# Sorting both token groups of the last feed-forward part into expert blocks, with one group's blocks between the steps of the second attention

## What is computed

```python
x = x + _L0_xattn_ref(_layernorm(x, axis=-1), ctx_1024, ...)   # 16 heads
x = x + _L0_ffn_ref(_layernorm(x, axis=-1), ...)               # 32 routed experts of width 64, dense, weighted
x = x + _L1_xattn_ref(_layernorm(x, axis=-1), ctx_1024, ...)   # one head of width 128
x = x + _L1_ffn_ref(_layernorm(x, axis=-1), ...)               # 8 experts, each token takes ONE of them

# _L1_ffn_ref
ids = jnp.argmin(_dist2(xn, centroids), axis=-1)
for e in range(N_EXPERTS):
    h = jnp.einsum('bsd,dh->bsh', xn, up_w[e])                  # 128 -> 512
    a, g = jnp.split(h, 2, axis=-1)
    y = jnp.einsum('bsh,hd->bsd', a * jax.nn.silu(g), down_w[e])
    out = jnp.where((ids == e)[..., None], y, out)
return out + skip
```

## Time and profile before

| | us |
|---|---|
| time, median of 3 runs | 336.48 (334.96 to 337.52) |
| the profiled execution, its time | 338.92 |
| its span, first to last instruction | 337.0 |
| PE busy | 275.8 (82%) |
| DVE busy | 217.7 (65%) |
| ACT busy | 153.2 (45%) |
| POOL busy | 150.9 (45%) |
| mean granted clock of PE | 0.915 |

### The profile page before, as it was taken

How to read it: one execution, slowest core, us unless ns; L and a number is a source line. 1 busy time by engine, 2 the same in 40 slices (tenths; PEclk the granted TensorE clock), 3 DMA queues, 4 the chain that set the end, 5 groups by cost and what they waited for, 6 DMA issues and landing times.

```text
span 337.0 us, 4616 instructions
## 1 busy us (share of the span) xinstructions
PE 275.8 (82%) x1501; PEld 178.9 (53%) x1525; DVE 217.7 (65%) x518; ACT 153.2 (45%) x277; POOL 150.9 (45%) x173
## 2 busy tenths in 40 slices
PE   3647897799999999797799969987997996924991
PEld 1422353344444454475477746866775774813861
DVE  4824688366568565688685694477779359641872
ACT  1110034444545666654655545843455853511550
POOL 6356024113112424087487763365645366470254
PEclk9975569999999999999999998997999998985896
DMA  6798936407410220284202100200000000015100
GB/s 194 221 139 208 196 103 167 85 10 182 69 58 0 68 81 3 52 72 115 64 2 62 46 18 0 63 1 0 0 4 0 0 2 0 0 64 177 43 12 11
DMA packets 13271, 21.85 MB, mean 65 GB/s; under 512 B 1709, under 2 KB 9841, under 8 KB 12736
## 3 DMA queue, kind: packets, MB, share of 16 engines
q1 hardware_dynamic: 10976, 14.46, 19.8%
q10 hardware_dynamic: 1728, 6.29, 6.6%
q0 software_dynamic: 544, 0.81, 0.7%
HBM read 18.32 MB, written 5.11 MB: 70 GB/s over the span
## 4 chain that ended last, share of the span: by engine, by line
PE 48%; DVE 17%; DMA 10%; POOL 10%; issue 7%; ACT 5%; SPq 2%; another core or an unknown queue 0%; ACTq 0%; DVEq 0%; POOLq 0%
PE psum L1170 43%; DMA big<-qk_scratch 4%; DMA qk_scratch<-parts 3%; DVE negmax L1084 2%; DVE early L1103 2%; DVE xn L969 2%; DVE early L1109 2%; DMA pvT<-mask_k 2%; POOL out L595 2%; POOL parts L580 2%; POOL big L580 1%; ACT early L733 1%; POOL row_blocks L590 1%; DVE stats L796 1%; DMA early<-row_blocks 1%
## 5 line engine op out<-in xcount | busy, mean ns | idle before, releaser
L1170 PE MATMUL psum<-xs,ws 128*128 128x512 f32 x192 | 56.7, 432 | 0.0
L1103 DVE TENSOR_TENSOR early<-early,psum 128x512 f32<-128x512 f32 x48 | 32.7, 682 | 36.6 <-ACT early L733 36.5
L1084 DVE TENSOR_REDUCE negmax<-psum 128x4 f32<-128x1024 f32 x32 | 39.1, 1221 | 23.3 <-PE psum L1170 23.2
L733 ACT ACTIVATE early<-psum 128x512 f32<-128x512 f32 x48 | 28.8, 600 | 48.4 <-PE psum L1170 48.3
L580 POOL TENSOR_TENSOR parts<-early,parts 128x512 fp32r<-128x512 f32 x24 | 31.0, 1290 | 41.5 <-ACT parts L725 41.4
L695 ACT ACTIVATE early<-psum 128x1024 f32<-128x1024 f32 x32 | 32.7, 1024 | 31.9 <-PE psum L1170 31.9
L1170 PE MATMUL psum<-maskb,id 128*128 128x512 bf16 x115 | 39.6, 421 | 4.8 <-DVE negmax L1084 3.5
L1170 PEld LDWEIGHTS psum<-big 32*128 32x128 f32 (+1 forms) x256 | 21.0, 203 | 38.9 <-issue 30.0
L1170 PE MATMUL psum<-big 32*128 32x256 f32 (+1 forms) x256 | 35.0, 355 | 7.7 <-DMA big<-qk_scratch 7.7
L1170 PEld LDWEIGHTS psum<-xs,ws 128*128 128x128 f32 x192 | 36.7, 197 | 7.9 <-issue 0.7
L1109 DVE TENSOR_TENSOR early<-early,psum 128x512 f32<-128x512 f32 x48 | 33.0, 687 | 3.2 <-POOL big L580 1.6
(11 more groups left out here) (226 smaller groups left out, 500.4 us busy)
## 6 DMA issues: line engine op xcount, KB each, us to landing
raw<-experts ACTq DMA_DIRECT2D x12, 512.0 KB, 3.8
big<-qk_scratch SPq DMA_DIRECT2D x24, 128.0 KB
qk_scratch<-parts SPq DMA_DIRECT2D x16, 128.0 KB, 2.8
row_blocks<-fill SPq DMA_DIRECT2D x1, 1452.0 KB, 24.6
early<-row_blocks SPq DMA_DIRECT2D x1, 1056.0 KB, 5.7
big<-qk_scratch SPq DMA_DIRECT2D x16, 64.0 KB
early<-sel SPq DMA_DIRECT2D x2, 512.0 KB, 7.6
ropet<-rope SPq DMA_DIRECT2D x2, 256.0 KB, 4.8
```

The lines of the kernel that those rows point to most:

```text
L733: nc.scalar.activation(sg[:, n % 2, :], psum[:, n % 2, :], ACT.Silu).then_inc(silu_ready, 1)
L1084: nc.vector.tensor_reduce(negmax[:, b % 2, :, :].rearrange("p t (r j) -> p r t j", r=2)[:, :, :, j], psum[:, bank:bank + 2, :].rearrange(" ...
L1103: nc.vector.tensor_tensor(sg[:, n % 2, :], sg[:, n % 2, :], psum[:, 2 + n % 2, :], ALU.mult).then_inc(up_read, 1)
L1170: return nc.tensor.matmul(o, w, r, start=start, stop=stop, skip_group_check=True)
```

## The change

The 16 dense units of the last part of g0 are gone: N_DENSE is 32. Both groups are sorted now, and two sets of 11 blocks follow.

- In g1's units (n = 16..31) stands the second attention of g0, now with `rank` and four scatters behind it (SECOND, now in half units: 2u before the down product, 2u+1 after it). norm2 and norm3 stand in the same unit as the task with their statistics, where they stood one unit later.
- g0's blocks come after unit 31; between them, by BESIDE_BLOCKS, stands the whole second attention of g1, its rank and its scatters. Then g1's blocks. A block's turned tokens are made four blocks at a time (xb0, xb1, xb2).
- Two scratch tensors row_blocks, so two fills, issued one behind the other where the one stood. POOL issues 22 output scatters instead of 11; the plain store of g0's result is gone.
- Splits 12 to 23 stand in every second unit (n = 1, 3, 5, ..., 23), so that all weights are there before the blocks. The parts of the hidden values have three rooms instead of four.

```diff
-DENSE = ((0, 0), (0, 1), (1, 0))
-N_DENSE = len(DENSE) * UNITS
+N_DENSE = GROUPS * UNITS
...
+LATE_ROOMS = 18
...
-SECOND = {"yT": 3, "norm2": 4, "k1proj": 4, "xT3": 5, "q1": 6, "s1": 7, "s1_": 7, "pT": 8, "pT_": 8, "pv1": 9,
-          "oproj1": 10, "norm3": 11, "skip": 12, "xT4": 12, "dist": 13, "ohT": 14}
+SECOND = {"yT": 6, "k1proj": 7, "norm2": 7, "xT3": 9, "q1": 10, "s1": 11, "s1_": 11, "pT": 13, "pT_": 13, "pv1": 14,
+          "oproj1": 16, "norm3": 17, "skip": 18, "xT4": 19, "dist": 21, "rank": 24, "rows0": 27, "rows1": 28, "rows2": 29,
+          "rows3": 30}
+
+BESIDE_BLOCKS = ({"yT": 0, "xb0": 0, "norm2": 0, "k1proj": 1, "xT3": 2, "xb1": 3, "q1": 3, "s1": 4, "s1_": 4, "xb2": 5, "pT": 6,
+                  "pT_": 6, "pv1": 7, "oproj1": 8, "norm3": 9, "skip": 10, "xT4": 11, "dist": 12, "rank": 14, "rows0": 15,
+                  "rows1": 15, "rows2": 15, "rows3": 15},
+                 {"xb0": 0, "xb1": 1, "xb2": 3})
...
-        row_blocks = nc.dram_tensor("row_blocks", [BLOCKS * P, ROW], F32, kind="Internal").ap()
+        row_blocks = [nc.dram_tensor(f"row_blocks{g}", [BLOCKS * P, ROW], F32, kind="Internal").ap() for g in range(GROUPS)]
...
+        late = sb("late", [P, 4096])
+        raw = late[:, 0:2048].rearrange("p (a n) -> p a n", a=2)
...
+            if n % 3 < 2:
+                return parts[:, 1024 * (n % 3):1024 * (n % 3 + 1)].rearrange("p (l t) -> p l t", l=2)
+            if n < LATE_ROOMS:
+                return we[:, :, 3 * CHUNK - GT:3 * CHUNK]
+            return xs[:, :, 0:GT]
...
-            sp.dma_start(row_blocks, fill.to_broadcast([BLOCKS * P, ROW])).then_inc(filled, 16)
-            sp.wait_ge(rows_out, 64)
-            blocks_of = row_blocks.rearrange("(j p) c -> p j c", p=P)
-            sp.dma_start(row_blk[:, 0:3, :], blocks_of[:, 0:3, :]).then_inc(blocks_in0, 16)
-            sp.dma_start(row_blk[:, 3:BLOCKS, :], blocks_of[:, 3:BLOCKS, :]).then_inc(blocks_in1, 16)
-            sp.wait_ge(y0_added, 1)
-            sp.dma_start(out[0:GT, :].rearrange("(t p) d -> p t d", p=P), acc[:, 0:4, :]).then_inc(out_done, 16)
-            sp.wait_ge(out_done, 16)
+            for g in range(GROUPS):
+                sp.dma_start(row_blocks[g], fill.to_broadcast([BLOCKS * P, ROW])).then_inc(filled, 16)
+            for g in range(GROUPS):
+                sp.wait_ge(rows_out, 64 * (g + 1))
+                blocks_of = row_blocks[g].rearrange("(j p) c -> p j c", p=P)
+                sp.dma_start(row_blk[g][:, 0:4, :], blocks_of[:, 0:4, :]).then_inc(blocks_in[g][0], 16)
+                sp.dma_start(row_blk[g][:, 4:BLOCKS, :], blocks_of[:, 4:BLOCKS, :]).then_inc(blocks_in[g][1], 16)
...
+                if name.startswith("rows"):
+                    t = int(name[-1])
+                    if t == 0:
+                        pool.wait_ge(filled, 16 * GROUPS)
+                        pool.wait_ge(acc4_ready, b + 1)
+                        pool.wait_ge(place_ready, b + 1)
+                    nc.gpsimd.indirect_dma_start(row_blocks[b], bass.IndirectOffsetOnAxis(ap=place_i[:, b, t:t + 1], axis=0),
+                                                 row_tok[:, t, :], None).then_inc(rows_out, 16)
...
-                    if wi < 24 and n % 3 == 1 and (wi < 22 or n > 2 * UNITS + DOWN_LAG):
+                    if wi < 24 and n % 2 == 1:
...
+            for at in range(2 * (BLOCKS + 2)):
+                for name, b in block_tasks(0, at):
+                    late_task(name, b)
+            for g in range(GROUPS):
+                pool.wait_ge(token_ready, g + 1)
+                for j in range(BLOCKS):
+                    pool.wait_ge(blk_out, BLOCKS * g + j + 1)
...
-                if i == 22:
-
-                    act.wait_ge(y_done, 2 * UNITS)
-                ws = (ws0 if c < 3 else ws1)[:, c % 3, :, 512 * q:512 * (q + 1)]
+                if i == 23:
+
+                    act.wait_ge(y_done, LATE_ROOMS)
...
-                if n >= 4:
-                    act.wait_ge(y_done, n - 3)
+                if n >= 3:
+                    act.wait_ge(y_done, n - 2)
...
+            for g in range(GROUPS):
+                weight_at = None
+                for i in range(BLOCKS + 2):
+                    for task in block_tasks(g, 2 * i):
+                        misc_task(*task)
+                    if i == 0:
+                        weight_at = weights_of(g)
+                    if i < BLOCKS:
+                        block_up(g, i, weight_at[i])
+                    if 1 <= i <= BLOCKS:
+                        hidden_turned(BLOCKS * g + i - 1)
+                    for task in block_tasks(g, 2 * i + 1):
+                        misc_task(*task)
+                    if i >= 2:
+                        block_down(BLOCKS * g + i - 2, weight_at[i - 2])
```

More of the change, by code:

```diff
@@ L62 @@
 UP_W, DOWN_W = 2 * HID, 2 * D
+EXPERT_W = UP_W + DOWN_W
+LATE_ROOMS = 18
 SM = {}
@@ L83, in misc_uses @@
         uses += [t for t in slot_tasks(s) if t[0] in MISC_READER]
-    for stage, g in DENSE:
-        for u in range(UNITS):
-            uses += [t for t in unit_tasks(stage, g, u) if t[0] in MISC_READER]
+    for n in range(2 * N_DENSE):
+        uses += [t for t in unit_tasks(n // 2, n % 2) if t[0] in MISC_READER]
+    for g in range(GROUPS):
+        for at in range(2 * (BLOCKS + 2)):
+            uses += [t for t in block_tasks(g, at) if t[0] in MISC_READER]
     return uses
@@ L124, in tail_tasks, with unit_tasks, block_tasks @@
     return [(name, b) for name, at in TAIL.items() if s == PAIRS * b + B_START + PAIRS + 1 + at]
-def unit_tasks(stage, g, u):
-    tasks = []
-    if stage == 0 and g == 0:
-        for b in range(B):
-            tasks += tail_tasks(SLOTS + u, b)
-    if (stage, g) in ((0, 1), (1, 0)):
-        tasks += [("rank" if (name, g) == ("ohT", 0) else name, g ^ 1) for name, at in SECOND.items() if u == at]
-    return tasks
+def unit_tasks(n, late):
+    g, u = n // UNITS, n % UNITS
+    if g == 0:
+        return [task for b in range(B) for task in tail_tasks(SLOTS + u, b)] if late else []
+    return [(name, 0) for name, at in SECOND.items() if at == 2 * u + late]
+def block_tasks(g, at):
+    return [(name, g if name.startswith("xb") else 1) for name, when in BESIDE_BLOCKS[g].items() if when == at]
 def misc_index(task):
@@ L361, in build @@
         for u in range(UNITS):
-            for name, b in unit_tasks(0, 0, u):
+            for name, b in unit_tasks(u, 1):
                 if name == "oproj":
@@ L578, in _ @@
+            for n in range(N_DENSE):
+                for late in range(2):
+                    for name, b in unit_tasks(n, late):
+                        late_task(name, b)
                 if n < LOW_ON_DVE:
@@ L738, in _ @@
                     hidden_high(n - 1)
-                if u == DOWN_LAG - 1 and n > UNITS:
-                    k = n // UNITS - 1
-                    act.wait_ge(y_done, UNITS * (k + 1))
-                    if k >= 1:
-                        act.wait_ge(misc_full, misc_index(("yT", k - 1)) + 1)
+                if n == UNITS + DOWN_LAG - 1:
+                    act.wait_ge(y_done, UNITS)
                     nc.scalar.copy(yT[:, :], psum[:, 5, :]).then_inc(y_evicted, 1)
-                for name, b in unit_tasks(stage, g, u):
-                    misc_task(name, b)
+                for late in range(2):
+                    for name, b in unit_tasks(n, late):
+                        misc_task(name, b)
@@ L1444, in hidden_turned, with weights_of @@
-            def hidden_turned(j):
-                pe.wait_ge(blk_hid, j + 1)
-                if j >= 2:
-                    pe.wait_ge(blk_hlo, j - 1)
+            def weights_of(g):
+                pe.wait_ge(weight_ready, g + 1)
+                return nc.values_load_multi_w_load_instructions(
+                    weight_i[0:1, g, :], engines=(mybir.EngineType.PE,), min_val=0, max_val=(E1 - 1) * EXPERT_W,
+                    skip_runtime_bounds_check_because="clamped to the last expert where it is stored")[1]
@@ L1481, in weights_at @@
-            def weights_at(which, top):
-                return nc.values_load_multi_w_load_instructions(weight_i[0:1, which, :], engines=(mybir.EngineType.PE,),
-                                                                min_val=0, max_val=top,
-                                                                skip_runtime_bounds_check_because="clamped to the last expert before it is stored")[1]
-            up_at, down_at = weights_at(0, (E1 - 1) * UP_W), weights_at(1, (E1 - 1) * DOWN_W)
-            pe.wait_ge(hidden_ready, N_DENSE)
```

441 lines of the change are left out of this document (196 added, 245 removed).

## The result

The changed kernel takes 356.51 us at the median of four runs (354.98 to 358.18), the kernel before beside it 337.0 us (334.96 to 337.63): a ratio of 1.059, with a 95% interval from 1.052 to 1.066. It is slower by 5.9%. The profiled execution spans 353.8 us, where that of before spans 337.0.

What follows compares the result with a forecast made beforehand. PE's dense units (busy 48.1 of 53.3 us) with the second-attention chain beside them; span 337.0 + 4.3 - 6.9 = 334.4, plus 27 for the load's wait, 361.4; median about 361, said 360, range 338 to 367.

Steps and rivals of the forecast that it cites:

- Half 7 is wanted at silu of n = 5 and lands late: g0's units: ACT waits for this expert half behind silu of n = 5; silu of n = 6 at least 5.3 us late.
- Until empty: Fill queue served until empty: half 7 lands at 181.8, silu of n = 6 26 us late, +27 in all; chance 0.43.
- the first rival: Engine takes turns at a DMA's end: half 7 lands at 160.8, half 8 about 181.8; median 350; chance 0.25.
- +4.3 for g1's units: n = 16 to 31: DVE sits through POOL's inverse root for norm2 and norm3, and rank keeps DVE; +4.3 us.
- 12 us to g0's first block: From the last unit: 12 us instead of 14.65, rank known three units earlier but scatters delay POOL's lo(28) to lo(30).
- 33 + 4 us from g0's first block to the places: g1's second attention beside g0's blocks: 33 us, the middle between 25 and 40.8, plus 4 us for half clock.
- 12 us from the places to g1's first block: Behind g1's sort: 12 us instead of 13.1, of which 1.1 came from POOL being still at work.
- g1's blocks, "the same": From g1's first block to the end: 28.85 us, as before.
- Sum of the rest of the chain, -6.9: Last unit of stage one to g1's first block: 61 us instead of 67.9; span without the load 334.4.
- Half clock through g0's blocks: PE's clock stays at half through g0's blocks: +7 us on any case; no case of its own, range top widened.
- "No wait, the sort pays": Half 7 is there by 153 us: kernel at 334, or 326 with the chain at its lower bound; chance 0.20.
- POOL's 22 outputs, no term: End of kernel: outputs at 1.46 us each end at 331, 3 us before the end; 2 us if POOL falls behind.

Runs made afterwards that it cites:

- experiment 1: Changed kernel with both fills of row_blocks issued only when the last expert half has landed: ratio 1.041 to the kernel before, 353.7 us.
- Experiment 7: Changed kernel, both fills late: second attention's norm2 and norm3 one unit behind their statistics, ratio 1.048; or xT3 half a unit and xT4 one unit later, 1.039.
- experiment 8: Changed kernel with two low-part products left out of g0's blocks, single run: 52.6 us from g0's first block to g1's, 56.9 in the changed kernel beside it.
- experiment 5: Changed kernel run again unchanged, ratio 1.073 (367.0 us), and with one SP wait that delays nothing, 1.082 (366.4 us); both take 101 us behind the last unit.
- experiment 6: Changed kernel without g0's 11 output DMAs (single run, 73.6 us from g0's first block to PE's last product), or with five issued earlier (76.7 us, ratio 1.069).

## Why the prediction was right, and where not

The forecast time, 360 us, was 3.5 us high and the direction right, but the case that I had called likeliest did not happen. The one that did had a chance of 0.25 and a forecast of 350. That 360 came closer is luck, since errors cancel. Of the span (361.4 forecast, 353.8 measured) the fills' waits were 11.2 us shorter than forecast, the start of the units 1.8 us earlier and g1's blocks 2.7 us shorter; the rest of g1's units was 1.9 us longer and the way from the last unit to g1's first block 6.2 us longer: -7.6 in all.

- **Half 7 is wanted at silu of n = 5 and lands late**: right. Issue 139.67 (forecast 141.5), the wait on ACT, the idle of DVE and of PE behind it, all at the named places.
- **"Until empty"**: wrong. The step that failed is "I take this, because in the one case the trace has, the load got nothing at all until the fill ran out". With one fill in the queue that case could not tell the end of a DMA from the end of the queue. Half 7 landed at 160.1, half 8 at 180.3, as the first rival said (160.8 and 181.8). The rule on packets of at most 64 that the prediction put beside this rival would have let half 7 through earlier, as with the cut fills 13 us after its issue; with whole fills it took 20. That rival's sum, +15.8 for both waits with their half clock, met the stretch to n = 19 exactly, but partly by luck: experiment 1 gives 12.6 of it to the fills, and 3.2 stay without them.
- **+4.3 for g1's units**: 6.2 in the profile. The mis-sized term is PE's idle time, which I had seen as DVE sitting through POOL's inverse root. Experiment 7 shows it isn't: PE comes to xT3 and xT4 with less work in hand, and more room there only moves the wait on.
- **12 us to g0's first block**: 13.35 (260.40 to 273.75), of which PE waits 3.94 for the read-back.
- **33 + 4 us from g0's first block to the places**: 39.3 (273.75 to 313.06). The two norms in quiet took 345 ns an instruction as expected. It fell near the upper of the bounds, 25 and 40.8: seven blocks in place of ten dense units and faster norms took only 1.5 us from the chain. A third less work for the blocks gives 1.3 to 1.8 us (experiment 8).
- **12 us from the places to g1's first block**: 14.6 (313.06 to 327.67). The four scatters were no slower than before (5.9 us from the places to the end of the last, 6.8 before). The read-back up to the first transposes took 5.5 us (4.8), and from there to the first block it took 3.2 us where it had been 1.5, with the rows of four blocks turned ahead of it instead of two.
- **g1's blocks, "the same"**: 26.1 instead of 28.85.
- **Sum of the rest of the chain, -6.9**: it was -0.7 up to g1's first block. The forecast 334.4 us for a kernel without the waits would have been some 341 by the first profile (353.8 less 12.7); the profile of experiment 1 spans 353.2, with 8 us more behind the last unit.
- **Half clock through g0's blocks**: the clock was 0.78 there, between the two cases. No run separates what it cost, so the 4 us in the sum are neither confirmed nor refuted.
- **"No wait, the sort pays"** fell twice: the wait came, and without it (experiment 1) the kernel is 4.1% slower, some 2% of it the loss of experiment 5 that the first profile did not have.
- **POOL's 22 outputs, no term**: right in the first profile. Whether they have a part in the 7 to 8 us that later profiles lose is open (experiment 6).

## What to carry to other kernels

A rival's reading of a single case is worth its price: one fill ahead of one load says nothing about two. Before adding a large DMA without a deadline, list what the other queues want from its issue on for twice its length; here, moving it to where nobody loads gave back 12.7 us in the units, and the way from there to PE's last product was as long as in the changed kernel run again (93.9 and 93.5 us). Replacing dense work by less work pays only where that work was the bound: from the last unit of g1 to the first block of its last part, 11 blocks instead of 16 units took 8.8 us of busy time from PE (52.5 to 43.7; 15.6 us at full clock), and the stretch became 0.7 us shorter. The attention chain, with the blocks between its steps, sets its length. And before two variants are ranked, one of them should be run again with an edit that changes nothing: here that alone moved the ratio by 1%.

## What the runs showed of the hardware

- A load that is issued behind a fill in another queue gets no packet until the first engines are through with that fill: its first came when 1352 to 1371 of 1424 had been moved. When the same bytes were cut into pieces of 144 packets, its first came after 948 to 973, over six pieces, so a queue keeps the engines over several small DMAs.
- One and the same program took 72.3 us from g0's first block to PE's last product in one profile and 80.5 in another, with PE's results reaching ACT about 3 us late (328.44 instead of some 325.6) in the second. Fewer indirect DMAs in a row on POOL went with less of it, but two profiles with all 15 had none at g1's first block: the cause is open.
- The same kernel stood at 1.059 times the kernel before on one occasion and at 1.073 on another, and beside the latter, with an edit that changes nothing, at 1.082, each time with intervals apart.
